# Attention's first ten steps of maxima split between three engines, its last ten steps' exponentials 1024 wide

## The reference, cut to what matters

```
query = heads(ct_q @ Wu_q + b) + heads(rope(ct_q @ Wq_r + b))      # key alike; value = heads(ct_kv @ Wu_v + b)
attn = jnp.einsum('bhqd,bhkd->bhqk', query, key) / scale
attn = softmax(attn, axis=-1)
out = jnp.einsum('bhqk,bhkd->bhqd', attn, value)
```

## Time and profile before

| | us |
|---|---|
| runs, median of 3 (lowest to highest) | 1261.92 (1258.29 to 1263.23) |
| the profiled execution | 1255.22 |
| its span | 1253.4 |
| PE, DVE, ACT busy in the span | 1061.6, 938.9, 780.5 |
| attention, first maximum to last copy of `acc` | 347.49 to 971.08 |
| granted clock of PE over the span | 0.926 |

### The profile page before, as it was taken

One profiled execution on the slowest core, in us unless ns is written; L12 is line 12 of the kernel. 1 busy time (PEld: TensorE's weight loads), 2 busy tenths in 40 slices (PEclk: granted clock), 3 DMA queues, 4 the chain that ended last, 5 costly groups with the idle time before them and its releaser, 6 DMA issues. The chain is left out here.

```text
span 1253.4 us, 23783 instructions
## 1 busy us (share of the span) xinstructions
PE 1061.6 (85%) x9052; PEld 507.1 (40%) x9052; DVE 938.9 (75%) x1445; ACT 780.5 (62%) x1539; POOL 323.2 (26%) x464
## 2 busy tenths in 40 slices
PE   6886789577779999999999999999998997179737
PEld 4785689433302222222222222222222974157315
DVE  7976244477799999999999999999990873046216
ACT  4544233144408999999999999999999452025101
POOL 4632548566410000000000000000000707700630
PEclk9998889798958999999999999999999988579959
DMA  7011466249960122112222201212000071211212
GB/s 225 1 35 35 122 169 182 90 55 209 235 116 2 33 32 32 22 14 33 32 33 33 32 6 29 33 32 33 2 3 2 12 186 45 53 30 60 59 33 59
DMA packets 94439, 76.92 MB, mean 61 GB/s; under 512 B 43220, under 2 KB 73300, under 8 KB 93816
## 3 DMA queue, kind: packets, MB, share of 16 engines
q1 hardware_dynamic: 89464, 65.42, 23.3%
q0 software_dynamic: 4864, 10.00, 3.5%
HBM read 47.77 MB, written 27.54 MB: 60 GB/s over the span
## 5 line engine op out<-in xcount | busy, mean ns | idle before, releaser
L1465 DVE TENSOR_REDUCE mx<-p_psA 128x1 f32<-128x1024 f32 x512 | 585.1, 1216 | 8.4 <-PE p_psA L1628 8.4
L1556 ACT ACTIVATE p_pt<-p_psS 128x512 f32<-128x512 f32 x1024 | 548.1, 596 | 36.8 <-PE p_psS L1650 17.1
L1663 PE MATMUL p_acc<-p_pt,V 128*32 128x256 f32 x4096 | 327.9, 392 | 15.4 <-ACT attn L1547 13.8
L1628 PE MATMUL p_psA<-K,Q 48*128 48x512 bf16 x1024 | 319.3, 394 | 9.4 <-DVE mx L1465 7.8
L1650 PE MATMUL p_psS<-Q,K 51*128 51x512 bf16 x1024 | 309.5, 384 | 0.0
L1663 PEld LDWEIGHTS p_acc<-p_pt,V 128*32 128x32 f32 x4096 | 81.8, 108 | 210.6 <-ACT p_pt L1556 110.5
L1628 PEld LDWEIGHTS p_psA<-K,Q 48*128 48x128 bf16 x1024 | 57.0, 94 | 232.3 <-DVE mx L1465 198.3
L1382 POOL TENSOR_TENSOR mr<-zeros,mx 128x16 f32<-128x16 f32 x32 | 7.1, 223 | 545.8 <-DVE mx L1465 545.8
L1932 DVE TENSOR_TENSOR f_part<-f_bank,mod 128x512 f32<-128x512 f32 x7 | 4.8, 692 | 97.9 <-remote 89.3
L1650 PEld LDWEIGHTS p_psS<-Q,K 51*128 51x128 bf16 x1024 | 62.6, 93 | 18.1 <-ACT p_pt L1556 12.6
L1894 PE MATMUL f_bank<-wsd,f_m 128*128 128x128 f32 x224 | 34.1, 295 | 41.1 <-issue 41.1
(11 more groups left out here) (343 smaller groups left out, 1474.4 us busy)
## 6 DMA issues: line engine op xcount, KB each, us to landing
f_w<-in_w SPq DMA_DIRECT2D x40, 256.0 KB
Q<-q_rows SPq DMA_DIRECT2D x32, 192.0 KB, 4.8
K<-k_rows SPq DMA_DIRECT2D x32, 192.0 KB, 5.3
result<-f_shared_kept SPq DMA_DIRECT2D x11, 256.0 KB, 2.3
result<-f_y SPq DMA_DIRECT2D x10, 256.0 KB
V<-v_rows SPq DMA_DIRECT2D x16, 144.0 KB, 5.7
hrows<-h SPq DMA_DIRECT2D x4, 516.0 KB, 7.7
x<-in_x SPq DMA_DIRECT2D x4, 512.0 KB, 5.5
```

Of the source, the lines that this page charges most:

```text
L1465: dve.tensor_reduce(mx[v % 2][:, h, qt:qt + 1], psA[t][:], AX.X, ALU.max).then_inc(a_max, 1)
L1556: act.activation(pt[s % 2][:, head_at(s, j), :], psS[k % 3][:], ACT.Exp, scale=INV_SCALE).then_inc(s_out, 1)
L1628: mm = pe.matmul(psA[t][:, c * 512:(c + 1) * 512], Q[g % NBUF][rows, pair, q0:q0 + P], K[g % NBUF][rows, pair, c * 512:(c + 1) * 512], sta ...
L1663: mm = pe.matmul(acc[VW * h:VW * (h + 1), cols], V[g % NBUF][:, kc, h * (HD + 1):h * (HD + 1) + VW], pt[s % 2][:, h, cols], start=(kc == 0 ...
```

## The change

`FAST` = 10 steps of maxima (20 maxima) are found in another way, from max(a, b) = a + relu(b - a). PE makes the product with the upper 512 keys and adds the product with the negated lower 512 (`nk`, made by two DVE instructions at the start) in the same bank; ACT takes the relu into SBUF (`excess`); PE makes the lower 512 keys' product in another bank; one DVE instruction adds the two 512-column tiles and takes the maximum (`tensor_tensor_reduce`, which the compiler turns into two: the operation itself and a 128x1 read-out of its result). Four slots are in flight, in six banks of PSUM. The other maxima stay as they are. `AHEAD` goes from 13 to 12. `turn(v+1)` moves from the end of step 8v+4 to the middle of step 8v+5, and ACT's copy behind the second exponential of that step. In the last ten steps (`WIDE0` = 246 on) the scores go to `psA`, which is free by then, and ACT takes two exponentials of 1024 columns a step instead of four of 512.

```
+        excess = [pt[1][:, i, :] for i in range(SLOTS)]
+        lower = [psA[0][:, 0:512], psA[1][:, 0:512], psS[0][:], psS[2][:]]
+        upper = [psA[0][:, 512:L], psA[1][:, 512:L], psS[1][:], acc[:]]
...
+                    dve.tensor_scalar(nk[rows, :, :], K[0][rows, :, 0:512], -1.0, None, ALU.mult).then_inc(nk_ready, 1)
+                for s in range(FAST):
+                    for t in range(2):
...
+                        dve.wait_ge(a_mm, i + 1)
+                        dve.wait_ge(r_ready, i + 1)
+                        dve.tensor_tensor_reduce(out=excess[n], in0=lower[n], in1=excess[n], scale=1.0, scalar=-3.0e38,
+                                                 op0=ALU.add, op1=ALU.max, accum_out=mx[s // KC][:, h, qt:qt + 1]).then_inc(a_max, 1)
...
+                def above(i):
+
+                    act.wait_ge(d_mm, i + 1)
+                    if i >= SLOTS:
+                        act.wait_ge(a_max, fast_before(i))
+                    act.activation(excess[FAST_SLOT[i]], upper[FAST_SLOT[i]], ACT.Relu).then_inc(r_ready, 1)
...
+                    for t in range(2 if s >= WIDE0 else 0):
+                        act.wait_ge(w_mm, 2 * (s - WIDE0) + t + 1)
+                        act.activation(pt[s % 2][:, 2 * t:2 * t + 2, :].rearrange("p h t -> p (h t)"), psA[t][:], ACT.Exp,
+                                       scale=INV_SCALE).then_inc(w_out, 1)
...
-                    if c == 0 and s >= 1:
-                        pe.wait_ge(a_max, 2 * (s - 1) + t + 1)
+                    if c == 0:
+                        pe.wait_ge(a_max, 2 * (s - 1) + t + 1 if s > FAST else (20, 18)[t])
...
+                    if part == 0:
+                        if i >= SLOTS:
+                            pe.wait_ge(r_ready, fast_before(i))
...
+                        pe.matmul(upper[FAST_SLOT[i]], q, high, start=True, stop=False)
+                        return
+                    if i < 2:
+                        pe.wait_ge(nk_ready, i + 1)
+                    pe.matmul(upper[FAST_SLOT[i]], q, minus_low, start=False, stop=True).then_inc(d_mm, 1)
...
+                    if i >= SLOTS:
+                        pe.wait_ge(a_max, fast_before(i))
+                    pe.matmul(lower[FAST_SLOT[i]], q, low, start=True, stop=True).then_inc(a_mm, 1)
...
-                        if t == 1 and s % KC == TURN and s // KC + 1 < NUNITS:
+                        if t == 0 and s % KC == TURN and s // KC + 1 < NUNITS:
                             turn(s // KC + 1)
```

More of the change, by code:

```diff
@@ L1166 @@
 GSTEPS = 2 * KC
-AHEAD = 13
-TURN = 4
+AHEAD = 12
+FAST = KC + 2
+SLOTS = 4
+FAST_SLOT = (*range(SLOTS),) * 4 + (0, 1, 3, 0)
+TURN = 5
 NSTEPS = NGRP * GSTEPS
 NUNITS = NSTEPS // KC
+WIDE0 = NSTEPS - AHEAD + 2
 NBUF = 3
@@ L1209, in score_at, with fast_before @@
 def score_at(s, j):
-    return 1 + s * QUAD + j + min((s + KC - 1 - TURN) // KC, NUNITS - 1)
+    return 1 + s * QUAD + j + min((s * QUAD + j + (KC - TURN) * QUAD - 2) // (KC * QUAD), NUNITS - 1)
 def turn_at(v):
-    return 0 if v == 0 else score_at((v - 1) * KC + TURN, QUAD - 1) + 1
+    return 0 if v == 0 else score_at((v - 1) * KC + TURN, 1) + 1
+def fast_before(i):
+    return max((n + 1 for n in range(i) if FAST_SLOT[n] == FAST_SLOT[i]), default=0)
 def head_at(s, j):
@@ L1547, in evacuate @@
                     act.activation(M.attn[:, u, :], acc[:], ACT.Copy).then_inc(acc_out, 1)
+                def above(i):
[3 more added lines that the diff above has]
+                    act.activation(excess[FAST_SLOT[i]], upper[FAST_SLOT[i]], ACT.Relu).then_inc(r_ready, 1)
+                for i in range(2 * FAST):
+                    above(i)
                 turned(0)
@@ L1557, in _ @@
                                        scale=INV_SCALE).then_inc(s_out, 1)
+                        if j == 1 and s % KC == TURN and s // KC + 1 < NUNITS:
+                            turned(s // KC + 1)
                     if s % KC == 0 and s >= 1:
                         evacuate(s // KC - 1)
[L1560 to L1561 removed]
                 evacuate(NUNITS - 1)
@@ L1652, in scores, with wide_scores @@
                               start=True, stop=True).then_inc(s_mm, 1)
+                def wide_scores(s, t):
+                    g, half, kc, i = s // GSTEPS, (s % GSTEPS) // KC, s % KC, 2 * (s - WIDE0) + t
+                    if kc == 0 and t == 0:
+                        pe.wait_ge(m_in[half], (g + 1) * 32)
+                    if i < 2:
+                        pe.wait_ge(a_max, 2 * NSTEPS)
+                    else:
+                        pe.wait_ge(w_out, i - 1)
+                    for r in range(2):
+                        rows = slice(64 * r, 64 * r + KROWS + MROWS)
+                        mm = pe.matmul(psA[t][:, r * 512:(r + 1) * 512], K[g % NBUF][rows, t, kc * P:(kc + 1) * P],
+                                       Q[g % NBUF][rows, t, half * 512:(half + 1) * 512], start=True, stop=True)
+                    mm.then_inc(w_mm, 1)
                 def values(s, part):
                     g, kc = s // GSTEPS, s % KC
-                    if part == 0:
+                    if part == 0 and s >= WIDE0:
+                        pe.wait_ge(w_out, 2 * (s - WIDE0) + 2)
+                    elif part == 0:
                         pe.wait_ge(s_out, score_at(s, QUAD - 1) + 1)
@@ L1666, in values @@
                     mm.then_inc(pv_done, 1)
-                for s in range(AHEAD):
+                for s in range(FAST):
+                    for part in range(2):
+                        for t in range(2):
+                            first_difference(s, t, part)
+                    for t in range(2):
+                        first_lower(s, t)
+                turn(0)
+                for s in range(FAST, AHEAD):
                     for t in range(2):
@@ L1671, in _ @@
                         a_part(s, t, 1)
-                    if s == KC:
-                        pe.wait_ge(full_ready[1], NM)
-                        turn(0)
                 for s in range(NSTEPS + 1):
+                    if s >= WIDE0:
+                        for t in range(2 if s < NSTEPS else 0):
+                            wide_scores(s, t)
+                        for part in range(2):
+                            values(s - 1, part)
+                        continue
                     for t in range(2):
```

36 lines of the change are left out of this document (28 added, 8 removed).

## The result

The changed kernel takes 1250.18 us, the median of six runs (1248.28 to 1256.15), beside 1262.07 for the kernel before in six of its own (1258.29 to 1263.23). The ratio is 0.9919 with a 95% interval of 0.9894 to 0.9945. By the ratio that is 10.2 us less (6.9 to 13.4 by the interval), by the medians 11.9, and faster by more than 0.5%. The two profiled executions are 5.0 us apart (1255.22 and 1250.26). Forecast was 1256. A second chip gave 0.9930 (0.9906 to 0.9954), an interval that reaches across 0.995.

The account below looks back on a forecast made before the run. Attention's ends were taken as bound by one engine each (DVE, then ACT), its middle by PE, DVE and ACT. Head -5.8, loop +2.3 and +1.3, tail -3.8 made -6.0 us: median 1256, range 1250 to 1264.

Parts of the forecast that it names:

- the forecast case: Whole kernel: every term stays within its bounds, giving 1252.5 to 1259 us; chance 0.47.
- head: From the first maximum to the first score: 24.2 us instead of 30.04, so -5.8, bounds -8.4 and -2.6.
- late landings: Loop: slow stores of maxima make PE wait 1.2 and 1.1 us if they come again; +1.3, kept 0 to 4.
- tail, wide steps: Last ten steps: 1024-column exponentials save 0.17 us a step, 1.7 in all, bounds 0 and 2.1.
- d: Head: time of each of the twenty fused maxima on DVE, taken as 0.80 us, bounds 0.67 and 0.96.
- from 2.35 on: Loop: a store of maxima costs time once its landing takes 2.35 us or more.
- The room: Loop: time from the turn to the next unit's first score, falling from 7.46 to 6.35 us, against a need of 5.4.
- late-turn rival: Loop: the turn is late in every unit, costing 31 x (need - 6.35); at need 6.85, 1270 us; chance 0.08.
- PE's chain of 1.99: Tail, wide steps: PE's next scores, values and first-half scores take 1.99 us a step, so 0.14 saved.
- dear fused maxima: Head: d is 1.0 to 1.25 us; at 1.2 the total is +2.0, 1264 us; chance 0.18.
- warm head: Head and loop start: PE's clock rises during the fused steps, saving 1.7, 0.4 and 0.2 us: 1253.7; chance 0.20.
- Wide steps give nothing: Tail: PE's chain is longer, so wide exponentials save nothing: 1258 us; chance 0.07.

Follow-up runs that it names:

- look-ahead and turn alone: The kernel before with look-ahead 12 and the turn in the middle of step 8v+5, nothing else; ratio 1.0008 (0.9995 to 1.0021).
- turn in mid-step, 13 ahead: The changed kernel with look-ahead 13, its turn left in the middle of step 8v+5; one run, 1159.89 us beside 1163.53 for the kernel before.
- all that helped: Against the kernel before: 12 fused steps, idle PE products in the head, 11 wide steps, look-ahead 13, old turn; 1148.76 us against 1165.83, ratio 0.9864.

## Why the prediction was right, and where it was not

The forecast was a median of 1256, 6.0 us less, in a range of 1250 to 1264. Measured was 1250.18. That is inside by 0.2 us, and below the 1252.5 at which the forecast case ended, so the number was met with luck. Of the three outcomes, "within 0.5%" had the largest chance (0.49), "faster" had 0.43, and it was faster. The forecast held for the stretches, where the change brought -7.0, and there too with luck: the head gained 3.8 more than forecast and the loop lost 3.3 more.

| step | forecast | measured |
|---|---|---|
| head | -5.8 | -9.6 |
| one more step in the loop | +2.3 | +2.3 |
| late landings | +1.3 | +2.1 |
| rest of the loop | 0 | +2.5 |
| tail, one step | -2.1 | -2.1 |
| tail, wide steps | -1.7 | -2.1 |
| sum (of the unrounded) | -6.0 | -7.0 |

- **The head: the mis-sized term is d.** The start was right: ACT's last piece ends at 349.99 and the first fused maximum comes at 350.63, forecast 350.75. d was taken as 0.80 and measured 0.61, and 20 x 0.19 is 3.8 us, which is the whole gap. The prediction put the floor at 0.67, the pitch of the similar instruction, and laid the read-out on top. It doesn't come on top (its start is that of the next maximum), and the pitch of another kind of instruction was no floor: the measured head lies 1.2 below the lower bound that was named. The return to the plain kind was 364.07 - 362.86 = 1.21, forecast 1.22. From there to the first score it took 3.64, forecast 3.74.
- **PE and ACT did keep up** with an even faster DVE: the twenty have an even pitch. But it was close. PE's 1.28 a step, forecast as about 1.3 against 1.6, was more than DVE's 1.22, and PE was busy 10.54 of the first 11.0. It had a lead, and the clock rose before that was used up.
- **The loop's step**: 2.3, as forecast.
- **Late landings.** The mechanism was right: stores up to 2.28 cost next to nothing, those of 3.32 and 3.24 cost 1.13 and 0.96, where the prediction's "from 2.35 on" gives 0.97 and 0.89. The room was 6.42, forecast 6.35. What was mis-sized is the term for how often: such landings were seen twice before, and a little over half their price was taken in case they stayed away. They came in every one of the twelve traces, one to three in 32. With the turn in mid-step at this room they cost 2.1 us (the kernel after), 1.7 (its second chip), 1.1 (look-ahead and turn alone) and 2.1 (turn in mid-step, 13 ahead).
- **"Nothing in a plain step's work changes."** It did. The turn in mid-step costs 0.06 to 0.07 in every unit, 1.9 us, which the turn's place alone shows (its loop of 18.53 a unit at 13 steps ahead). It is not the load's landing. ACT is 0.06 to 0.07 us further behind PE in mid-step: the last exponential ahead of the turn ends 1.04 after it instead of 0.97, and the copy begins 0.92 after it instead of 0.86. The second score behind the turn waits for that exponential, and every half step behind it starts later by that much. The reason given against the late-turn rival, that ACT is as close behind PE in mid-step as at a step's end, was off by this. Why ACT is further behind there stays open.
- **The slow start.** 8.1 us for two and a half steps, where before it was 6.2 for two: about 0.8 us more (worked out at 2.32 a step). It scatters: the same kernel had 8.1 and 11.8 on its two chips.
- **The tail.** The step saved 2.1. The wide steps saved 0.21 a step, the upper bound: the prediction lengthened ACT's 1.92 to PE's chain of 1.99, which was wrong, as ACT's idle time before its twenty instructions is 0.6 us in all while PE waits for ACT. The parts that the prediction names for the chain add up to 1.93 and not to 1.99, and PE was in fact done within ACT's 1.90. The figures of the Trainium skill, ScalarE: Activation LUTs, section "What ACT_TABLE_LOAD costs", give an estimate of 0.946 for this pitch, and the rows here show 0.951.

The rivals: *dear fused maxima* fell at 0.61. The *warm head* had its condition and not its gain: the clock did rise during the fused steps (0.93 from 358.3 to 362.3, when PE had been busy 10.54 of the 11 us ahead), but it was back at 0.50 in the plain maxima, where PE was busy 3.13 of 5.40, and the loop started slow. The prediction's reason against it was off, as PE was busy 3.00 of 4.00 at 0.93 and not under half. What it left out is the plain maxima between the fused steps and the loop. With extra products there, the clock gave 3.3 us, where the prediction had 2.3: the head's part was 0.6 as forecast, the loop's 2.7 instead of 1.7, against a slow start that was longer than before's (8.7, not 6.2). *Wide steps give nothing* fell at 0.21 a step.

What stays open: by the ratios the change is worth 10.2 and 8.1 us on the two chips, by attention in the profiles 7.0 and 5.9. The stretch ahead of attention is 0.2 shorter in the kernel after and the one behind it 1.9 longer, and both intervals hold 7 (6.9 to 13.4 and 5.4 to 11.0). The rest is not explained, and may be scatter. What makes some stores land late was not settled either.

## What to carry to other kernels

When a step is moved within a loop, price its place in every turn of the loop, even if it has room: here 0.06 us times 31 ate nearly all of the 2.1 that the shorter look-ahead gave in the head and the tail together, net of its step in the loop. An event that a trace shows twice in 32 is part of the kernel, and counts with its full price unless a run shows that it stays away. Where an instruction isn't in the trace, the pitch of a similar one is an estimate and no bound, so keep the range open below it too. And read what a late transfer costs from how late the waiting instruction comes, not from the idle time listed at it.

## What the runs showed of the hardware

- A fused maximum over 512 columns, one tile from PSUM and one from SBUF, has a length of 0.69 us and a pitch of 0.61. Its read-out (0.08) starts together with the next such instruction and costs nothing while they follow each other.
- The store of the turned maxima lands after 1.37 us in most units, and in each of the twelve traces one to three of 32 took 2.6 to 3.63.
- In the dense loop PE's granted clock was 0.56 and 0.60 in the 3.9 and 4.3 us behind idle times of 1.96 and 1.42 us, and 1.00 before and after. Behind an idle time of 1.18 it stayed at 1.00 (all in the kernel with the turn at the end of step 8v+5).
- With 56 idle products between the last fused maxima and the loop (40 in the kernel with all that helped) the granted clock stayed at 1.00 into the loop. Without them it was 0.50 (1.2 GHz) there. The 60 ahead of the fused steps did not keep it up: it was 0.50 from 344.5 to 350.4.
